# A decoder with routed experts on one core: three stages in one block instead of four blocks, and the first expert weights asked for when the table is written

## What is computed

```
x = layernorm(x + nystrom_attention(x));  x = layernorm(x + dilated_attention(x, ctx))
x = layernorm(x + ternary_ffn(x));        x = layernorm(x + (x + fast_weight_memory(x)))
x = layernorm(x + relu(lin(layernorm(x + gated_cross_attention(x, ctx)) * gamma + beta)))
top, ids = top2(x @ Wg + bg);             gate = softmax(top)
y = x + sum over the two experts e in ids of (silu(gate*x @ W1[e]) * (gate*x @ W3[e])) @ W2[e]
y = layernorm(x + y)
```

## Time and profile before

| | |
|---|---|
| median of 3 runs | 1747.32 us (1746.74 to 1750.34) |
| the profiled execution | 1735.48 us |
| its span, first to last instruction | 1733.7 us |
| TensorE's mean granted clock | 0.897 of full |
| busy: PE, DVE, ACT, POOL | 83%, 68%, 42%, 19% of the span |
| HBM read, written | 115.62 MB, 33.05 MB |

### The profile page before, as it was taken

The page is one execution under the profiler, slowest core; times in us unless marked ns, Lnnn a source line. Parts: engine busy times, 40 slices in busy tenths (PEclk is TensorE's granted clock), DMA queues, the critical chain, the costliest instruction groups (busy, mean ns, idle before and its releaser), DMA issues. The chain is left out here.

```text
span 1733.7 us, 46403 instructions
## 1 busy us (share of the span) xinstructions
PE 1436.0 (83%) x19772; PEld 1188.6 (69%) x19772; DVE 1182.7 (68%) x2581; ACT 725.8 (42%) x1451; POOL 335.4 (19%) x340
## 2 busy tenths in 40 slices
PE   4997895699889577989877799889563999999993
PEld 3985773489667356976654589577343888888882
DVE  5776675666756846685684757667654788888874
ACT  3213433232244333214334331343324777777771
POOL 0002130210303102020230210213011232332332
PEclk8799997879999797999998789999786999999996
DMA  6331120000000001000000100000005777877764
GB/s 267 129 133 70 50 74 7 26 27 4 2 3 7 19 1 51 3 3 2 1 25 2 37 16 3 2 2 1 1 20 202 225 226 231 235 226 228 233 171 110
DMA packets 51413, 133.30 MB, mean 77 GB/s; under 512 B 5121, under 2 KB 30721, under 8 KB 50177
## 3 DMA queue, kind: packets, MB, share of 16 engines
q1 hardware_dynamic: 40009, 114.58, 19.7%
q0 software_dynamic: 8160, 10.49, 3.2%
q10 hardware_dynamic: 3040, 5.25, 0.8%
HBM read 115.62 MB, written 33.05 MB: 86 GB/s over the span
## 5 line engine op out<-in xcount | busy, mean ns | idle before, releaser
L2138 PE MATMUL m_bank<-e_xT,e_w 128*128 128x256 bf16 x2208 | 248.1, 275 | 4.8 <-DVE e_w L2222 4.2
L2138 PEld LDWEIGHTS m_bank<-e_xT,e_w 128*128 128x128 bf16 x2208 | 217.6, 99 | 32.0 <-issue 4.5
L704 PEld LDWEIGHTS bank<-arena 64*64 64x64 f32 x6400 | 220.3, 142 | 12.9 <-issue 7.7
L704 PE MATMUL bank<-arena 64*64 64x80 f32 (+2 forms) x6400 | 226.3, 231 | 3.3 <-DVE arena L843 1.8
L2222 DVE TENSOR_TENSOR e_w<-e_raw,e_w 128x1024 bf16<-128x1024 f32 x138 | 166.8, 1223 | 54.8 <-ACT e_w L2171 54.7
L1023 POOL TENSOR_TENSOR rstd<-ve,neghalf 128x2 f32<-128x2 f32 x48 | 37.4, 778 | 716.7 <-DVE ve L1001 715.9
L2171 ACT CAST e_w<-e_raw 128x1024 bf16<-128x1024 f32 x138 | 141.7, 1043 | 17.9 <-DMA e_raw<-E 17.9
L2153 PE MATMUL m_bank<-e_w,e_h 128*128 128x256 bf16 x1104 | 124.1, 273 | 0.0
L2153 PEld LDWEIGHTS m_bank<-e_w,e_h 128*128 128x128 bf16 x1104 | 108.0, 98 | 12.2
L967 ACT COPY arena<-bank 128x320 f32<-128x320 f32 (+1 forms) x96 | 37.6, 392 | 159.8 <-PE bank L704 159.4
L2241 DVE TENSOR_TENSOR e_h<-m_bank,e_silu 128x256 f32<-128x256 f32 x184 | 77.3, 420 | 32.8 <-ACT e_silu L2188 32.8
(11 more groups left out here) (298 smaller groups left out, 2838.0 us busy)
## 6 DMA issues: line engine op xcount, KB each, us to landing
e_raw<-E SPq DMA_DIRECT2D x138, 512.0 KB, 4.8
slots<-C_empty SPq DMA_DIRECT2D x13, 1360.0 KB
e_x<-slots SPq DMA_DIRECT2D x23, 272.0 KB, 5.9
w_rest<-W_rest SPq DMA_DIRECT2D x1, 3592.0 KB, 16.6
xz<-xT SPq DMA_DIRECT2D x8, 256.0 KB, 2.6
x<-x SPq DMA_DIRECT2D x8, 256.0 KB, 3.2
ctx<-ctxT SPq DMA_DIRECT2D x8, 256.0 KB, 2.7
tokens<-y SPq DMA_DIRECT2D x8, 256.0 KB, 2.1
```

Of the source, the lines that this page charges most:

```text
L704: last = pe.matmul(b[r, p * width:(p + 1) * width], lhs[r, 4 * g + p, :], rhs[r, 4 * g + p, :], start=True, stop=True)
L2138: last = pe.matmul(bank[b][:, col:col + wide], w13[u][:, wp, which, c, f * P:(f + 1) * P], xeT[u][:, xp, c, 0:wide], start=j == 0, stop=j ...
```

## The change

The two kernels' functions become functions that return one program per engine (`layers_programs`, `experts_programs`), and `build` opens a single block in which each engine runs its part of the layers, of the experts and of the final norm. Block 2 is gone. Since nothing is cleared, semaphores cannot be reused, and they are made fewer: one counter where there were several (the six norms of a stream, the pieces' splits, the columns' turns). A counter's value stands for the same event as before. The experts use the layers' PSUM banks, the final norm uses the layers' constant -0.5. DVE's last table instruction raises a semaphore `table`; SP waits for it, asks for pieces 0 to 3 of tile 0, and only then waits for `m_sent` and `stored` ahead of rows(0). `hidden(0)` waits for its four pieces one at a time, where each is used first. The rooms that routing and stores still read (`slot_rows`, `y0`, `y1`, `m_*`) now lie outside what the experts' buffers take over.

The diff, whitespace ignored, cut:

```diff
-            dve.tensor_copy(shared["row"][:], start[:, 2])
+            dve.tensor_copy(shared["row"][:], start[:, 2]).then_inc(sem("table"), 1)
...
-                for s in range(STREAMS):
-                    sp.wait_ge(sem(f"stored{s}"), 16 * batches)
-                for s in range(STREAMS):
-                    sp.wait_ge(sem(f"m_sent{s}"), 16 * TOPK * NT * batches)
...
-        with nc.Block() as block:
-
-            @block.sync
-            def _(sp):
-                for x in list(sems.values())[0::5]:
-                    sp.sem_clear(x)
...
+        def await_tokens_stored(engine):
+            for s in range(STREAMS):
+                engine.wait_ge(sem(f"stored{s}"), due("stored", BATCH, 0))
+        def await_rows_sent(engine):
+            for s in range(STREAMS):
+                engine.wait_ge(sem(f"m_sent{s}"), due("m_sent", BATCH, 0))
+        def await_table(engine):
+            engine.wait_ge(sem("table"), 1)
...
-        bank = [ctx.enter_context(nc.psum_tensor(f"m_bank{i}", [P, 512], F32)) for i in range(8)]
+    bank = layers.psum
...
-        split_high = [sem(f"e_weights_high{q}") for q in range(PIECES_OF_TILE)]
-        split_low = [sem(f"e_weights_low{q}") for q in range(PIECES_OF_TILE)]
+    split_high, split_low = sem("e_weights_high"), sem("e_weights_low")
...
-        turns = lambda i, f: 2 * i + f // 4 + 1
+    column = lambda i, f: FE * i + f + 1
+    order_of_splits = [(0, q) for q in range(4)]
+    for i in range(TILES):
+        order_of_splits += [(i + 1, q) for q in range(4) if i + 1 < TILES] + [(i, q) for q in (4, 5)]
+    done_pieces = lambda i, q: order_of_splits.index((i, q)) + 1
...
+        layers.await_table(sp)
                 weights(0, (0, 1, 2, 3))
+        layers.await_rows_sent(sp)
+        layers.await_tokens_stored(sp)
                 rows(0)
                 rows(1)
...
-                    pe.wait_ge(te[u], nth(i))
-                    for q in range(4):
-                        pe.wait_ge(split_low[q], i + 1)
+            pe.wait_ge(te, i + 1)
+            if i:
+                pe.wait_ge(split_low, done_pieces(i, 3))
...
+                        if i == 0 and f == 0 and j % len(TERMS) == 0:
+                            pe.wait_ge(split_low, done_pieces(0, 2 * which + c))
...
-                    for b in range(4):
-                        pe.wait_ge(hl[b], turns(i, 4))
-                    for q in (4, 5):
-                        pe.wait_ge(split_low[q], i + 1)
+            pe.wait_ge(hl, column(i, FE - 1))
+            pe.wait_ge(split_low, done_pieces(i, 5))
...
-        with nc.Block() as block:
-            @block.gpsimd
-            def _(pool):
-                pool.memset(half[:], -0.5).then_inc(halved, 1)
-                pool.wait_ge(halved, 1)
+    def pool_final(pool):
...
-        layers_kernel(nc, {**a, "y": tokens, "slots": slots, "sums": sums}, shared)
-        experts_kernel(nc, {**a, "x5": tokens, "slots": slots, "y": y}, shared)
+        layers = layers_programs(nc, {**a, "y": tokens, "slots": slots, "sums": sums}, shared, ctx)
+        experts = experts_programs(nc, {**a, "x5": tokens, "slots": slots, "y": y}, shared, ctx, layers)
+
+        with nc.Block() as block:
+            @block.sync
+            def _(sp):
+                layers.sp(sp)
+                experts.sp(sp)
```

More of the change, by code:

```diff
@@ L4 @@
 from concourse.alu_op_type import AluOpType as ALU
+from collections import namedtuple
 from contextlib import ExitStack
@@ L403, in sem @@
             if name not in sems:
-                sems[name] = ctx.enter_context(nc.semaphore(name))
+                sems[name] = kept.enter_context(nc.semaphore(name))
             return sems[name]
@@ L416, in side_by_side @@
             return whole, views
+        slot_rows = sb_kept("slot_rows", [P, STREAMS, TOPK, NT, WIDE_ROW])
+        y_rooms = [sb_kept(f"y{s}", [P, NT, D]) for s in range(STREAMS)]
+        routing = [{n: sb_kept(f"m_{n}{s}", [P, *shape], kind) for n, (kind, *shape) in ROUTED.items()} for s in range(STREAMS)]
+        NEGH = shared["neghalf"]
         W, whole_W = {}, {}
@@ L461, in layers_kernel @@
                  "ve": sb(f"ve{s}", [P, NT]), "rstd": sb(f"rstd{s}", [P, NT])}
-            v["m"] = {n: sb(f"m_{n}{s}", [P, *shape], kind) for n, (kind, *shape) in ROUTED.items()}
+            v["m"] = dict(routing[s])
             v["m"]["rows"] = slot_rows[:, s]
@@ L1006, in dve_norm @@
                                          ALU.subtract, ALU.mult)
-            last.then_inc(sem(f"x{key}_{s}"), 1)
+            last.then_inc(sem(f"normed{s}"), 1)
         def dve_residual_norm(dve, bat, link, name, key):
@@ new lines, in sp_layers, with pe_layers, dve_layers, link @@
+        def sp_layers(sp):
+            sp_first(sp)
+            merged(sp, [stream(s, (sp_gated,), sp) for s in range(STREAMS)] + [nothing(), sp_clear(sp)], merge_order(ORDERS["sp"]))
+        def pe_layers(pe):
+            layers = (pe_nystrom, pe_dilated, pe_ffn, pe_memory, pe_gated)
+            merged(pe, [stream(s, layers, pe) for s in range(STREAMS)] + [nothing(), nothing(), routers(pe_router, pe)], merge_order(ORDERS["pe"]))
+        def dve_layers(dve):
+            links = 0
+            dve_link = sem("dve_link")
+            def link(ins):
+                nonlocal links
+                links += 1
+                ins.then_inc(dve_link, 1)
+                dve.wait_ge(dve_link, links)
+            layers = (dve_nystrom, dve_dilated, dve_ffn, dve_memory, dve_gated)
+            merged(dve, [stream(s, layers, dve, link) for s in range(STREAMS)] + [nothing(), dve_setup(dve), routers(dve_router, dve, link)], merge_order(ORDERS["dve"]))
+            dve_table(dve, link)
@@ L2383, in build, with _ @@
         shared = {n: ctx.enter_context(nc.sbuf_tensor("s_" + n, shape, kind))
-                  for n, shape, kind in (("expert", [P, TABLE], I32), ("row", [P, TABLE], I32), ("ident", [P, P], F32))}
+                  for n, shape, kind in (("expert", [P, TABLE], I32), ("row", [P, TABLE], I32), ("ident", [P, P], F32), ("neghalf", [P, NT], F32))}
         sums = nc.dram_tensor("sums", (P, 2), F32, kind="Internal").ap()
-        layers_kernel(nc, {**a, "y": tokens, "slots": slots, "sums": sums}, shared)
-        experts_kernel(nc, {**a, "x5": tokens, "slots": slots, "y": y}, shared)
+        layers = layers_programs(nc, {**a, "y": tokens, "slots": slots, "sums": sums}, shared, ctx)
[5 more added lines that the diff above has]
+                experts.sp(sp)
+            @block.tensor
+            def _(pe):
+                layers.pe(pe)
+                experts.pe(pe)
+            @block.vector
+            def _(dve):
+                layers.dve(dve)
+                experts.dve(dve)
+            @block.scalar
+            def _(act):
+                layers.act(act)
+                experts.act(act)
+            @block.gpsimd
+            def _(pool):
+                layers.pool(pool)
+                experts.pool(pool)
 def kernel(**inputs):
```

662 lines of the change are left out of this document (310 added, 352 removed).

## The result

The change makes the kernel a little faster: 1744.09 us (median of 20 runs, 1737.88 to 1747.79) against 1750.47 us (median of 20 runs of the kernel before, 1746.42 to 1755.11), a ratio of 0.9965 with a 95% interval of 0.9954 to 0.9976. That is 6.4 us, where 11.0 had been forecast. The median of before is itself 3.2 us above that of the three runs shown ahead of the prediction, so the gain is read from the ratio, not from the distance to 1747.32.

The account below looks back on a forecast made before the run. PE, busy 83% of the span, was taken to bound the tiles end to end, so the gaps mattered: 8.8 + 2.2 = 11.0 us off the three-run median gave 1736.3 us, range 1732.0 to 1742.5.

Parts of the forecast that it names:

- the two gaps: Table's end to hidden(0), 21.9 us, and last matmul to first m_z load, 9.5 us; forecast to lose 8.8 and 2.2.
- Early request, traffic and last piece: After the table: first weight request 9.4 us earlier, 0.6 us lost to shared DMA traffic, last piece 8.8 us earlier.
- Let it slip by 0 to 3 us: SP's slot-row wait would end 0 to 3 us later; rows would still land behind the last weight piece.
- rival 1: Slot rows get stuck behind the early weights, giving back 2.8 to 4.8 us; 1740.1 us; chance 0.14.
- the first gap: From the table's end to hidden(0), 21.9 us with PE working 1.97; forecast to shrink by 8.8 us.
- 2.53 us after the transposes began: Before hidden(0): the time from PE's first transposes to hidden(0) was carried over unchanged as 2.53 us.
- First tile: Between hidden(0) and hidden(1): PE's 4.2 us wait for tile 1's fourth piece stays, and PE stays cold.
- Second gap: From PE's last matmul to the first m_z load, 9.5 us: request 2.2 us earlier, bounds 1.8 to 2.4.
- The same chain, 20.2 us: Final norm at the program's end: same chain of loads, DVE and stores, unchanged at 20.2 us.
- Merged semaphores and wait instructions: Across the kernel: shared counters make no one wait longer, and PE's seven fewer waits per tile save nothing.
- Rival 3: The layers run longer at the low clock, eating the gain: 1747 us, chance 0.09, or 1754 us, chance 0.07.

Follow-up runs that it names:

- e1_late: The changed kernel, but SP asks for no weights until the slot rows are written; 423.9 us after the table in its profile.
- e5_six: The changed kernel with all six pieces of tile 0 asked for ahead of the slot-row wait instead of four; 423.7 us after the table in its profile.
- e7r_regs: The changed kernel, with SP reading the two starting rows into registers before its slot-row wait; 423.2 us after the table in its profile.
- the g runs: Three kernels adding unread PE products, two on the change with POOL's drain before the final norm, one on f1_all; 420.9, 418.5, 416.3 us after the table.
- f1_all: The change plus POOL's drain before the final norm, rows read early, tile 1's transposes inside hidden(0), two tile 1 pieces requested sooner; 1739.97 us, ratio 0.9948.
- g3_all_warm: f1_all plus 58 unread PE products before hidden(0) and between hidden(0) and hidden(1); 1736.99 us, ratio 0.9909 to the kernel before.

## Why the prediction was wrong

The direction was right, and the two gaps did shrink, but 4.6 of the 11.0 us did not come (6.4 measured). Three steps failed: the slip of the wait for the slot rows, put at 0 to 3 us, was 4.4; the stretch from the transposes to hidden(0), carried over as 2.53 us, was 3.36; and the end of the program, taken as the same 20.2 us, was 22.35, since POOL's drain was put at nothing there.

1. **Early request, traffic and last piece: right.** Forecast was a first request 0.95 us after the table and a last piece 8.8 us earlier; it was 1.03 us, and 18.68 - 9.90 = 8.78.
2. **"Let it slip by 0 to 3 us": wrong.** The wait for the slot rows slipped by 4.4 us (back to nothing in e1_late), so PE's first transposes began at 12.05, not at 19.45 - 8.8 = 10.65: 1.40 us lost. This is rival 1, whose point of decision, a wait ending over 7 us after the table, was passed. Its mechanism was half right: the last row write stands behind two pieces in full, but not behind all four. That its total, 6.2 to 8.2 us left, holds the measured 6.4 is luck: the first gap lost 2.23 us of the forecast where the rival had 2.8 to 4.8, and the rest is POOL's drain (step 6), which no rival had. The argument against the rival, that the last row write is issued 0.6 us after the first request, judged by the time of issue: before the change too, with nothing beside it, that write's data began to move 1.5 us after its issue (3.1 us after the table), and the wait lasted until 4.0.
3. **"2.53 us after the transposes began": wrong.** It took 3.36, because the second `e_x`, which lands 0.5 to 1.3 us after PE is through with the first when both are asked for on an otherwise free ring, stands ahead of hidden(0) in PE's program. Before, both had landed behind the weights and PE did all eight transposes in one row. 0.83 us lost. Where PE did not have to wait for the second `e_x` the stretch was 2.52 us again (e1_late, e5_six, e7r_regs). Steps 2 and 3 make 2.23: 8.8 forecast, 6.57 measured.
4. **First tile: right as read, but the reading was shallow.** Hidden(1) followed by 16.54 us with 4.1 us of waiting, and 17 us of idleness instead of 24 left the clock at 0.50. I took both as given; the g runs show that 4.6 to 5.2 us lay there, which no part of the change touches.
5. **Second gap: right.** 2.2 us forecast, 2.34 measured.
6. **"The same chain, 20.2 us": wrong.** The chain up to the last store is the same; the program's end is not. Taking out block ends did not take out what their drains had paid for. POOL's drain grew from 892 to 6132 ns and passed ACT's end by 2.15 us. The forecast had priced POOL's drain twice as something removed and never asked where it would go.
7. **Merged semaphores and wait instructions: nothing, as forecast.** Hidden(0) to the last matmul takes 378.61 us, against 378.58.
8. **Rival 3, the layers at the low clock: not seen.** The table came 12 us later in the change's profile, but the layers' mean granted clock was 0.89 against 0.88, not lower. The table came between 1296.5 and 1321.6 us in programs with equal layers; why is open, and the medians' gain agrees with what the stages after the table lost.

The sum by the runs: 6.57 + 2.34 - 2.15 and under 0.1 of small change are 6.8 us in the profiles, 6.4 in the medians.

## What to carry to other kernels

When a block's end or a barrier is removed, list what it paid for (drains, clears) and where that falls due next; put a drain where its engine idles anyway. An early transfer helps only as far as the consumer's program order and the other queue's small writes allow: read both before pricing it. And where shortening one wait moves nothing, look for two limits that hide behind each other, such as a cold PE and a late piece; test them together as well as alone.

## What the runs showed that I had not expected

- POOL's DRAIN takes 0.89 us with no indirect DMA behind it, 4.65 with 46 and 6.13 with 78: some 46 ns more for each of the 32 row writes, though all had landed long before.
- A small scattered write issued while one, two, four or six 512 KB loads are being asked for on another queue lands 1.5, 3.3, 4.4 and 4.7 us later: the first two cost it their whole time, those behind them little more.
- The granted clock in the first 8 us of hidden(1), 0.65, 0.79 or 1.00, goes with 13.60, 12.58 or 10.92 us from hidden(1) to answer(0).
- Useless products on an idle PE brought the kernel from 0.995 to 0.991 of its time before (f1_all to g3_all_warm). The Trainium skill ("TensorE: Matmul & The Clock Gate", section "What's actually happening") puts the cost of a cold start under 1% of a typical span; the trace agrees, 4.5 of 1740 us being 0.26%, but here that was two thirds of what the change itself gained.
